# A four-layer graph network on one core: layer 2 aggregates h before the weights, in two fp16 parts, and the last gated step takes two tiles

## What is computed

```python
def _gcn_conv(x, edge_index, W, b):                 # layer 2
    h = x @ W
    msgs = h[src]
    agg = jax.ops.segment_sum(msgs, dst, num_segments=x.shape[0])
    return agg + b
def _graph_norm(x, weight, bias, mean_scale):
    mean = jnp.mean(x, axis=0, keepdims=True)
    xc = x - mean_scale * mean
    var = jnp.mean(xc * xc, axis=0, keepdims=True)
    return xc * jax.lax.rsqrt(var + EPS) * weight + bias
h  = relu(graph_norm(gcn_conv(x, W1, b1), ...)) + x
h2 = relu(graph_norm(gcn_conv(h, W2, b2), ...)) + h

gates = sigmoid(concat([h[src], h[dst], edge_attr]) @ W_e + b_e)      # layer 1
messages = softplus(concat(...) @ W_n + b_n)
h_new = segment_sum(gates * messages, dst); return h + h_new / edge_count
```

## Time and profile before

| | us |
|---|---|
| median of 3 runs | 2909.52 (2906.31 to 2911.4) |
| the profiled execution, its own time | 2907.12 |
| its span in the profile | 2905.4 |
| layer 1 ends, layer 2 begins (SP's first DMA) | 2294.16 |
| layer 2 ends, layer 3 begins (SP's first DMA) | 2565.78 |
| busy in the span: PE, PEld, DVE, ACT, POOL | 2412.0, 2165.6, 1660.3, 1387.1, 930.6 |

### The profile page before, as it was taken

One profiled execution on the slowest core, in us unless ns is written; L12 is line 12 of the kernel. 1 busy time (PEld: TensorE's weight loads), 2 busy tenths in 40 slices (PEclk: granted clock), 3 DMA queues, 4 the chain that ended last, 5 costly groups with the idle time before them and its releaser, 6 DMA issues. The chain is left out here.

```text
span 2905.4 us, 60492 instructions
## 1 busy us (share of the span) xinstructions
PE 2412.0 (83%) x19085; PEld 2165.6 (75%) x19086; DVE 1660.3 (57%) x3510; ACT 1387.1 (48%) x2794; POOL 930.6 (32%) x1143
## 2 busy tenths in 40 slices
PE   2877787777999999878888888888888497959998
PEld 1656566567999999678777777777777376749998
DVE  7776676665444444576666666666666624265455
ACT  2555565551333333245555555555555312037676
POOL 1222221210000000077777777777777100000000
PEclk6999999997999999955555555555555597969999
DMA  1333333330000000254444444444444430068271
GB/s 60 117 117 110 106 114 102 108 119 2 2 2 2 2 2 2 76 136 115 114 114 113 108 115 114 113 108 115 114 111 111 150 159 1 1 259 298 79 255 58
DMA packets 182762, 283.34 MB, mean 98 GB/s; under 512 B 73651, under 2 KB 150518, under 8 KB 177174
## 3 DMA queue, kind: packets, MB, share of 16 engines
q1 hardware_dynamic: 143670, 200.51, 21.7%
q0 software_dynamic: 38880, 79.68, 10.6%
HBM read 210.93 MB, written 69.15 MB: 96 GB/s over the span
## 5 line engine op out<-in xcount | busy, mean ns | idle before, releaser
L1143 POOL DMA_INDIRECT layer_R<-source_terms,layer_srcs x804 | 782.4, 973 | 244.9 <-issue 244.9
L1363 PE MATMUL layer_zp<-layer_right,layer_left 96*128 96x192 f32 x1350 | 479.5, 541 | 156.8 <-DVE layer_left L1162 154.7
L566 PE MATMUL build_win<-nodes_x,build_S 128*128 128x200 f16 x3948 | 426.9, 256 | 162.5 <-DVE nodes_x L487 147.2
L1363 PEld LDWEIGHTS layer_zp<-layer_right,layer_left 96*128 96x128 f32 x1350 | 412.1, 331 | 173.4 <-DVE layer_left L1162 166.8
L937 PE MATMUL layer_acc<-layer_U,graph_CT 128*128 128x192 f16 x6250 | 521.5, 246 | 20.7 <-DVEq L786 20.7
L937 PEld LDWEIGHTS layer_acc<-layer_U,graph_CT 128*128 128x128 f16 x6250 | 517.3, 98 | 28.2 <-issue 24.3
L566 PEld LDWEIGHTS build_win<-nodes_x,build_S 128*128 128x128 f16 x3948 | 318.6, 100 | 265.8 <-DVE nodes_x L487 186.6
L1383 PEld LDWEIGHTS layer_acc<-layer_hot,layer_G 128*98 128x98 f32 x1656 | 272.3, 272 | 113.7 <-DVE layer_aggT L1210 113.4
L1383 PE MATMUL layer_acc<-layer_hot,layer_G 128*98 128x32 f32 x1656 | 287.5, 342 | 51.5 <-DVE layer_aggT L1210 51.5
L1881 PE MATMUL layer_acc<-layer_V,layer_turn 128*128 128x96 f32 x2500 | 288.5, 278 | 0.6 <-issue 0.6
L1881 PEld LDWEIGHTS layer_acc<-layer_V,layer_turn 128*128 128x128 f32 x2500 | 286.6, 195 | 0.9 <-issue 0.9
(11 more groups left out here) (254 smaller groups left out, 3039.1 us busy)
## 6 DMA issues: line engine op xcount, KB each, us to landing
layer_ring<-W_blocks SPq DMA_DIRECT2D x41, 1600.0 KB, 7.4
W_blocks<-nodes_x SPq DMA_DIRECT2D x400, 100.0 KB, 1.8
layer_left<-in_attr SPq DMA_DIRECT2D x68, 384.0 KB
C_blocks<-build_Cblk SPq DMA_DIRECT2D x25, 800.0 KB, 4.7
layer_C<-C_blocks SPq DMA_DIRECT2D x25, 800.0 KB, 21.6
layer_R<-source_terms,layer_srcs POOLq DMA_INDIRECT x804
layer_rows<-target_rows SPq DMA_DIRECT2D x68, 96.0 KB
layer_right<-target_terms SPq DMA_DIRECT2D x136, 24.0 KB
```

Of the source, the lines that this page charges most:

```text
L566: mm = pe.matmul(out, S[:, b, part, 2 * i + u, :, :].rearrange("p a z -> p (a z)"), M[:, i, u, :, :].rearrange("p a z -> p (a z)"), start= ...
L1143: nc.gpsimd.indirect_dma_start(R[:, i, u, :], None, P_d, bass.IndirectOffsetOnAxis(ap=at_u, axis=0)).then_inc(s_R[i], 16)
L1363: pe.matmul(out[u], left[:, i, u * P:(u + 1) * P], right[:, i, :], start=(u % 2 == 0), stop=False, skip_group_check=True)
```

## The change

**Layer 1.** `TAIL` is the number of tiles of the last step, 806 - 134 * 6 = 2. Where a step's number is a constant (the steps behind the loop), `tiles(s)` says how many tiles are gathered, added, exponentiated and summed: 2 in step 134, 6 elsewhere.

**Layer 2** is written anew. Since A(hW) = (Ah)W, the counts now aggregate `h` and the product with `W` is taken for each target tile afterwards. `h` is scaled by powers of two (`HSCALE`, and `up` and `down` by column in the second convolution) and split into two fp16 parts: ScalarE makes the first by a copy (`high`), GpSimd the second, h minus the first (`low`), five tiles at a time. The layernorm works in five pieces of five tiles, its squares on ScalarE. PE takes the first six target tiles together, source tile by source tile, in six PSUM banks, then the others one after another; between the halves of a target tile it turns a finished aggregate (`turn`) and multiplies an older one by `W` (`weigh`), by a table `turn_plan()`. ScalarE and VectorE take an aggregate out in two instructions (`lows`, `whole`), VectorE adds the bias (`conv`). The columns and squares are no longer summed in a pass at the end: the mean of the first tile is subtracted from every tile, ScalarE squares each `cv` tile, GpSimd keeps running sums of both, and one product with `ones` and four small ones give the totals. The normalization then is two factors for a column and passes in pieces of 480 elements in the first convolution, three of 2400 in the second. The parameters get 2 more DMAs (`col`) behind the first six blocks of `C`; the blocks are waited for in groups of 6, 5, 5, 5 and 4. The multiplications of `h` by `up` and `down` and the addition of `h` to `x` lie in the aggregation, in tiles 13 to 17 (`spare`).

```diff
@@ gated_edges
+        def tiles(s):
+            return TAIL if isinstance(s, int) and s == NS - 1 else SE
-                for u in range(SE):
+                for u in range(tiles(s)):
@@
-                nc.scalar.activation(y[:, h, :, :], R[:, i, :, :], ACT.Abs).then_inc(s_abs, 1)
+                n = tiles(s)
+                nc.scalar.activation(y[:, h, 0:n, :], R[:, i, 0:n, :], ACT.Abs).then_inc(s_abs, 1)
@@ residual_gcn, GpSimd
+            def low(i, q):
+                t = piece(q)
+                pool.wait_ge(s_hi, 5 * i + q + 1)
+                nc.gpsimd.tensor_tensor(U[:, t, 1, :], h[:, t, :], U[:, t, 0, :], ALU.subtract).then_inc(s_U, 1)
+            for i in range(NL):
+                for q in range(5):
+                    low(i, q)
+                pool.wait_ge(s_cv0, i + 1)
+                for n in range(1, NT - 2):
+                    pool.wait_ge(s_sq, i * NT + n + 1)
...
+                    nc.gpsimd.tensor_tensor(total[:, 0, :], cv[:, 0, :] if n == 1 else total[:, 0, :], cv[:, n, :],
+                                            ALU.add)
+                    nc.gpsimd.tensor_tensor(total[:, 1, :], sq[:, 0, :] if n == 1 else total[:, 1, :], sq[:, n % SQ, :],
+                                            ALU.add).then_inc(s_sum, 1)
@@ residual_gcn, VectorE
+            def whole(i, n):
+                dve.wait_ge(s_lo, i * NT + n + 1)
+                nc.vector.tensor_tensor(agg[:, n % AB, :], agg[:, n % AB, :], acc[:, n % FIRST, 0:D],
+                                        ALU.add).then_inc(s_agg, 1)
+            def conv(i, n):
+                dve.wait_ge(s_pr, i * NT + n + 1)
+                nc.vector.tensor_tensor(cv[:, n, :], pr[:, 0:D], vec[:, 0 + i, 0, :] if n == 0 else rest_b,
+                                        ALU.add).then_inc(s_cv, 1)
+            def residual(q):
+                t = piece(q)
+                step(nc.vector.tensor_tensor(cv[:, t, :], cv[:, t, :], wide(mid), ALU.add))
+                nc.vector.scalar_tensor_tensor(h[:, t, :], cv[:, t, :], 0.0, h[:, t, :], ALU.max, ALU.add).then_inc(s_h, 1)
@@ residual_gcn, PE
+            def product(j, k):
+                return pe.matmul(acc[:, j % FIRST, 0:2 * D], C[:, j, k, :], U[:, k, :, :].rearrange("p a f -> p (a f)"),
+                                 start=(k == 0), stop=(k == NT - 1))
+            pe.wait_ge(s_C[0], 16 * FIRST)
+            for i in range(NL):
+                for q in range(4):
+                    pe.wait_ge(s_U, 5 * i + q + 1)
+                    for k in range(5 * q, 5 * q + 5):
+                        for j in range(FIRST):
+                            product(j, k)
...
+                for n in range(FIRST, NT):
+                    for half in range(2):
+                        outs, t = slots[n, half]
...
+                        for out in outs:
+                            weigh(i, out)
+                        if t is not None:
+                            turn(i, t)
...
+                            pe.wait_ge(s_agg, i * NT + n - FIRST + 1)
+                        for k in halves[half]:
+                            mm = product(n, k)
+                    mm.then_inc(s_acc, 1)
```

More of the change, by code:

```diff
@@ L1416, in _, with __init__, put, after @@
                     mm.then_inc(s_turn, 1)
+class Count:
+    def __init__(self, eng, sem):
+        self.eng, self.sem, self.n = eng, sem, 0
+    def put(self, ins):
+        self.n += 1
+        ins.then_inc(self.sem, 1)
+        return self.n
+    def after(self, n):
+        self.eng.wait_ge(self.sem, n)
+def turn_plan():
+    slots, turned, out = {}, 0, 0
+    for n in range(FIRST, NT):
+        for half in range(2):
+            ready = 0 if n == FIRST and half == 0 else max(FIRST - 1, n - 2 + half)
+            outs = [out] if out < turned and (n, half) != (FIRST + 1, 0) else []
+            turn = turned if turned <= ready else None
+            slots[n, half] = outs, turn
+            out += len(outs)
+            turned += turn is not None
+    return slots, out
 def residual_gcn(nc, x, ident, C_d, layers):
+    slots, last = turn_plan()
+    halves = (range(0, NT // 2), range(NT // 2, NT))
     with ExitStack() as ctx:
```

449 lines of the change are left out of this document (297 added, 152 removed).

## The result

The changed kernel takes **2804.3 us** (median of four, 2803.6 to 2806.2) against 2910.5 (median of four, 2906.3 to 2911.5): a ratio of **0.963**, 95% interval 0.962 to 0.964, 106.1 us less. The forecast was 2803, inside 2793 to 2825. The profiled execution took 2806.2 us (before 2907.1) with a span of 2804.5.

The account below looks back on a forecast made before the run. Layer 2's two aggregations were taken as bound by PE, its other stretches by hand-off chains through ScalarE and VectorE. 7.7 + 14.7 + 19.8 + 33.8 + 18.9 + 11.8 = 106.7 us less gave 2803 us, range 2793 to 2825.

Parts of the forecast that it names:

- end of layer 1: Layer 1's last step: no wait for the last gather and shorter instructions turn `aggT` 8.0 us earlier, taken as 7.7.
- start to first product: Layer 2's start: the sixth block of `C` sets PE's first product, 21.3 us instead of 36.0, 14.7 less.
- first aggregation: Layer 2, first convolution: 192-column products at 0.0834 us plus turns and weighings, 64.8 us instead of 84.6, 19.8 less.
- GraphNorm 1 to first product: Between layer 2's aggregations: small instructions, first piece and GpSimd's subtraction take 8.4 us instead of 42.2, 33.8 less.
- second aggregation: Layer 2, second convolution: like the first but with pieces 0.7 late, 65.5 us instead of 84.4, 18.9 less.
- GraphNorm 2 and end: Layer 2's end: small instructions, three passes and the barrier take 12.6 us instead of 24.4, 11.8 less.
- rival C: Layer 2's start: the 25 loads share the engines, six blocks do not land first; 2810 or 2839 us; 5%.
- 0.7 us for late pieces: Second aggregation's start: GpSimd's subtractions slow VectorE, pieces come every 3.2 us and the fifth is 0.7 late.
- no wait of PE over 0.1 us: Sign that the forecast is right: in the aggregations, 2.4 us from tile to tile without a longer PE wait.
- rival A: Aggregations: half a tile does not cover turns and weighings, PE waits at each; up to 24 us, 2827; 10%.
- Rival B: Second aggregation's restart: VectorE keeps GpSimd out until all five pieces are through; 7.8 us later, 2811; 10%.
- rival D: Both aggregations: small fp32 instructions keep PE's clock at 1.2 GHz; 116 us more, 2919, slower than before; 3%.

Follow-up runs that it names:

- Experiment 1: Changed kernel with layer 1's last gated step put back at its old six tiles (`TAIL = SE`); ratio 0.9664 to the kernel before.
- Experiment 5: Changed kernel with the ten parameter loads issued behind the first six blocks of `C`, not ahead; ratio 0.961, layer 2 172.2 us.
- experiment 6: Changed kernel with a semaphore for each of the first six blocks, first 150 products in arrival order, column loads ahead of `C`; ratio 0.9626, layer 2 174.5 us.
- experiment 2: Changed kernel with each of the 1250 aggregation products 288 columns wide instead of 192; ratio 0.9806, layer 2 221.5 us.
- experiment 3: Changed kernel with each weighing right behind its own tile's turning, no products between; ratio 0.969, layer 2 190.8 us.
- Experiment 8: Changed kernel with the second aggregation's low parts made by VectorE instead of GpSimd; ratio 0.9628 (one run), layer 2 172.3 us.
- experiment 10: Kernel of experiment 6 plus a semaphore for every block, with parameter and column loads moved behind the third block of `C`; ratio 0.9606, layer 2 166.2 us.

## Why the prediction was right

By its own steps, in the profile (the forecast's saving, what was measured):

| step | forecast | measured |
|---|---|---|
| end of layer 1 | 7.7 | 8.0 (21.48 to 13.52) |
| start to first product | 14.7 | 14.4 (36.0 to 21.6) |
| first aggregation | 19.8 | 18.4 (84.6 to 66.2) |
| GraphNorm 1 to first product | 33.8 | 34.1 (42.2 to 8.1) |
| second aggregation | 18.9 | 18.0 (84.4 to 66.4) |
| GraphNorm 2 and end | 11.8 | 12.1 (24.4 to 12.3) |
| sum | 106.7 | 105.0 |

The profiled executions differ by 100.9 us, as the later one lost 4.6 before the changed step; the medians differ by 106.1.

- **End of layer 1.** Right in both parts, the missing wait for the gather and the lengths by elements. Experiment 1 gives 8.1 us back when it is undone.
- **Start.** The model was that the sixth block's arrival sets it, and PE's first product comes at 21.6 us against 21.3. Experiment 5 shows that a load order moves it (14.4), and experiment 6 that block 0 is there 12.5 us after the start and block 1 two us later; rival C (all together) falls. That `scales` is covered was right: it ended about 27 us after the start.
- **Aggregation.** The 0.0834 us of a 192-column product taken from layer 0 held (low copies 0.41 apart for five products), and experiment 2 shows width to be the price. Both aggregations are 0.9 to 1.4 us over the forecast, in three of its terms. The first 150 products took 15.2, not 14.3, because PE ran at half clock for 5.8 us, not 3.6: the length of the cold part was read off a mean clock of a long stretch, and it differs from run to run (3.1 in experiment 1). The tail behind the last product is 3.2 us, not 2.8; four small column-sum products were counted as one. In the second aggregation the 0.7 us for late pieces did not come up, and the 1.5 us of the spare instructions were missing: the prediction summed VectorE's load of 0.6 us a tile and called it covered, but a hand-off needs VectorE and ScalarE at a certain moment, not on the mean. So one sign named for the forecast, no wait of PE over 0.1 us, did not hold at these tiles (0.26 in the row shown), though the forecast did. That is rival A's mechanism at a tenth of its price; experiment 3 gives its whole price, 16 us, where the prediction had bounded it at 24.
- **GraphNorm 1.** 8.1 against 8.4. The small instructions took 3.8 us, not 4.1, and GpSimd's subtraction 1.49, where 1.2 and 0.4 of waiting on VectorE had been put. Rival B falls: the subtraction starts 0.08 us behind ScalarE's copy, not after the fifth piece. The later pieces never came late, as they were 2.7 us apart and not 3.2 (1.2 had been added to the 2.0 in full, while VectorE stood still for only 0.77). This step and GraphNorm 2 are 46 of the 105 us, and no run puts them back; what they cost is read from the rows before and after alone.
- **Small slips and luck.** By the prediction's own terms, 24 turns and 23 weighings are 7.2 us, not 7.1, and a fifth piece at 12.8 us would be 1.0 behind the 120 products (10.0 and 1.8), not 0.7. The aggregations gave 2.3 us less than forecast and the other four steps 0.6 more in sum. As the cold parts alone move layer 2 by 1 or 2 us from run to run, it is in part luck that the median lies within 1.3 us of 2803.
- **GpSimd's part.** The prediction said that the subtraction on VectorE would be 0.66 and the change gives away some 1 us here. Experiment 8 shows 0.8 at the first product, and no slower pieces (one profile; the 2.3 us of the whole layer are mostly the clock's). The Trainium skill ("GPSIMD Engine Reference", "Engine selection") puts elementwise work on VectorE for its speed; here the runs agree, and for a stronger reason, that GpSimd's work also stops VectorE's.
- **The clock** (rival D) was at 2.4 GHz in both aggregations but for the starts (granted 1.00 over 2320.4 to 2378 and over 2390.5 to 2449); the small fp32 products between do not lower it.

## What to carry to other kernels

When a transfer feeds a stage, an earlier first product is worth nothing until the wait behind it has been looked up: kernel 6 gained 9 us at the start and lost them at the next semaphore, which counted five blocks together. Give each block a semaphore of its own (six in turn are enough for 25) before judging bandwidth.

A hand-off across three engines that is hidden under half a tile has a slack of a few tenths of a us. Work that is "free" on the mean load belongs there one piece at a time, and behind the instruction that someone waits for.

When an effect is smaller than the spread of unchanged stages, measure its own stretch: layer 2's length showed steps of some us while its start moved by 13. And go on until the stretch holds only what was edited: of the 2.3 us that layer 2 lost in experiment 8, 1.3 stood in code that was the same. In the same way look up what PE waits for before saying what bounds it: in experiment 10 the blocks, which were moved, had long stopped being the bound.

## What the runs showed of the hardware

- A GpSimd subtraction and VectorE instructions with two SBUF inputs hold each other up: 1.49 instead of 1.09 us for the one and 1.43 instead of 0.66 for the other. Handing 480 elements to GpSimd cost VectorE 0.77 us, more than the 0.66 of doing it.
- PE's clock came back between 2.7 and 5.3 us into the restart, after 8 us of idleness and with the same code. Products whose sums nobody reads count like any others for it: with 28 of them ahead the clock was 1.00 from the first product on, in two kernels. In one run it held through pauses of 1.95 and 0.96 us and fell 0.4 us after the second.
- The twelve small loads of a layer (eight of 48 KB, two of 36 KB, two columns) keep `C` from moving for about six us behind whichever blocks they are put: 46 to 101 GB/s in experiment 5 (2297 to 2303), 59 to 103 in experiment 10 (2296.8 to 2302.8), 400 and more behind. SP needs 4.6 us to issue ten of them, and their 0.47 MB would be 1.1 us at the blocks' rate.
- Block 1 came about 2 us behind block 0 (PE's products of it began 1.97 us later, at 419 to 426 GB/s), which is one block's bytes at that rate: blocks land in the order of issue.
